# Filler products between scores and values of a Taylor attention, and a DMA wait moved behind the third value store

## The reference

```
k_l = ctx @ Wk_l + bk_l        v_l = ctx @ Wv_l + bv_l        (4096 x 256, l = 0..3)
```

```
s = q.k / 4        weight = 1 + s + s*s/2        out = sum(weight * v) / (sum(weight) + 1e-12)
```

## Time and profile before

| | us |
|---|---|
| median of 3 runs | 1507.49 |
| lowest and highest | 1505.61, 1515.83 |
| the profiled execution's own time | 1513.84 |
| its span | 1512.6 |
| mean granted clock of TensorE in it | 0.958 of 2.4 GHz |

### The profile page before, as it was taken

One profiled execution on the slowest core, in us unless ns is written; L12 is line 12 of the kernel. 1 busy time (PEld: TensorE's weight loads), 2 busy tenths in 40 slices (PEclk: granted clock), 3 DMA queues, 4 the chain that ended last, 5 costly groups with the idle time before them and its releaser, 6 DMA issues. The chain is left out here.

```text
span 1512.6 us, 29029 instructions
## 1 busy us (share of the span) xinstructions
PE 1382.8 (91%) x10576; PEld 812.2 (54%) x10576; DVE 1011.3 (67%) x2314; ACT 857.3 (57%) x1308; POOL 566.7 (37%) x686
## 2 busy tenths in 40 slices
PE   8999798999999988699999888699999897999987
PEld 3765546355555456255555455245555582555555
DVE  4446384999999734778787043498885236888832
ACT  5144140899999721288888542167777211777762
POOL 4565242598989910656555331011111001111100
PEclk9999999799999988799999999889999997999999
DMA  8888987245547053266565094346776711567800
GB/s 265 287 270 247 258 231 246 50 64 85 75 71 155 2 81 44 53 91 88 85 85 144 19 223 171 105 64 102 106 104 209 108 18 45 92 99 105 157 2 8
DMA packets 126008, 178.30 MB, mean 118 GB/s; under 512 B 14733, under 2 KB 106021, under 8 KB 116646
## 3 DMA queue, kind: packets, MB, share of 16 engines
q1 hardware_dynamic: 111898, 161.04, 51.3%
q10 hardware_dynamic: 13968, 15.41, 3.4%
HBM read 132.58 MB, written 43.78 MB: 117 GB/s over the span
## 5 line engine op out<-in xcount | busy, mean ns | idle before, releaser
L1002 ACT ACTIVATE prob_a<-ps 128x1024 f32<-128x1024 f32 x464 | 456.4, 1020 | 143.0 <-PE ps L834 95.7
L817 PE MATMUL ps<-kop,qop 116*128 116x512 bf16 x1024 | 350.3, 406 | 37.3 <-DMA qop<-qparts 24.0
L1026 DVE TENSOR_REDUCE best_a<-ps 128x1 f32<-128x512 f32 (+1 forms) x488 | 318.6, 709 | 49.4 <-PE ps L817 48.9
L834 PE MATMUL ps<-qop,kop 116*128 116x256 bf16 x2048 | 333.9, 274 | 3.2 <-ACT prob_a L1002 2.6
L834 PEld LDWEIGHTS ps<-qop,kop 116*128 116x128 bf16 x2048 | 193.9, 98 | 123.2 <-ACT prob_a L1002 20.2
L1022 DVE CUSTOM_DVE_ANT_0 dump_a<-ps,neg_q 128x512 bf16<-128x512 f32 (+1 forms) x244 | 165.7, 715 | 43.9 <-PE ps L817 41.8
L861 PE MATMUL ps<-prob_a,vop_a 128*32 128x256 f32 x3072 | 191.7, 383 | 3.1 <-POOL prob_a L1166 2.2
L817 PEld LDWEIGHTS ps<-kop,qop 116*128 116x128 bf16 x1024 | 95.6, 103 | 167.0 <-issue 71.0
L1136 POOL TENSOR_TENSOR used_a<-prob_a,gT 128x1024 f32<-128x1024 f32 x64 | 153.1, 2393 | 23.7 <-DVE used_a L1039 18.2
L1115 POOL CAST mpart_a<-nmax_a 128x2 bf16<-128x2 f32 x64 | 26.3, 410 | 353.7 <-DVE nmax_a L1031 353.7
L1166 POOL TENSOR_TENSOR prob_a<-prob_a,neg_k 128x1024 f32<-128x1024 f32 x48 | 102.5, 2135 | 92.0 <-ACT prob_a L1000 86.5
(11 more groups left out here) (337 smaller groups left out, 1830.2 us busy)
## 6 DMA issues: line engine op xcount, KB each, us to landing
kop<-kparts SPq DMA_DIRECT2D x448, 128.0 KB, 5.1
kparts<-kp SPq DMA_DIRECT2D x64, 384.0 KB, 4.7
vals<-vst SPq DMA_DIRECT2D x16, 1024.0 KB, 5.2
vraw<-vals SPq DMA_DIRECT2D x64, 256.0 KB, 6.6
e_w<-in_e_w SPq DMA_DIRECT2D x4, 2048.0 KB, 11.1
z_w<-in_z_w SPq DMA_DIRECT2D x24, 256.0 KB, 6.8
ctxT<-in_ctxT SPq DMA_DIRECT2D x8, 512.0 KB, 8.0
raw<-in_mask ACTq DMA_DIRECT2D x16, 256.0 KB, 5.4
```

The lines of the kernel that those rows point to most:

```text
L817: return pe.matmul(out, qop[0:R_ALL, h, t * P:(t + 1) * P], kop[0:R_ALL, h % UNROLL, j * CHUNK:(j + 1) * CHUNK], start=True, stop=True)
L834: ins = pe.matmul(st_bank(n)[:, j * NT:(j + 1) * NT], kop[0:R_ALL, h % UNROLL, k * P:(k + 1) * P], qop[0:R_ALL, h, :], start=(j % 2 == 0), ...
L1002: act.activation(prob[:, n % NP, :], st_bank(n), ACT.Exp).then_inc(S("exp_done"), 1)
L1026: dve.tensor_reduce(out, bank, AX.X, ALU.max).then_inc(sem, 1)
```

## The change

In the Taylor attention five filler products are issued after scores(0), ahead of values(g) in each of the four rounds, and after the last turn_back, all into bank 0. In the projection stage SP's wait for the blind row's stores, and the load behind it, move from ahead of layer 2's first value store to behind its third.

```diff
-SOFTMAX_FILL, SCAN_FILL = 12, 12
+SOFTMAX_FILL, SCAN_FILL, GROUP_FILL = 12, 12, 5
...
-                if l == 2:
-                    sp.wait_ge(S("blind_stored"), 16 * QT)
-                    sp.dma_start(blind, c.blind_row.rearrange("n o -> o n").to_broadcast((P, NT))).then_inc(S("blind_loaded"), 16)
                 for n in range(NV):
                     b = NV * l + n
                     sp.wait_ge(S("v_staged"), KT * l + VB * (n + 1))
                     sp.dma_start(vout[l, :, n, :, :, :], vst[:, b % VSLOTS, :, :, :])\
                       .then_inc(S(f"v_stored{b % VSLOTS}"), 16)
+                    if l == 2 and n == NV - 2:
+                        sp.wait_ge(S("blind_stored"), 16 * QT)
+                        sp.dma_start(blind, c.blind_row.rearrange("n o -> o n").to_broadcast((P, NT))).then_inc(S("blind_loaded"), 16)
...
             scores(0)
+            keep_warm(c, pe, GROUP_FILL, 0)
             pe.wait_ge(S("v_ready"), 1)
             pe.wait_ge(S("vop_ones"), 1)
             for g in range(G):
                 if g + 1 < G:
                     scores(g + 1)
+                keep_warm(c, pe, GROUP_FILL, 0)
                 values(g)
                 if g >= 1:
                     turn_back(g - 1)
             turn_back(G - 1)
+            keep_warm(c, pe, GROUP_FILL, 0)
             pe.wait_ge(S("normalised"), G)
```

## The result

| | before | after |
|---|---|---|
| median of 20 runs, us | 1511.24 | 1505.64 |
| lowest and highest | 1504.58, 1518.33 | 1501.22, 1511.67 |
| profiled execution, span | 1512.6 | 1503.8 |
| mean granted clock in it | 0.958 | 0.968 |

The ratio of after to before is 0.9967, 95% interval 0.9953 to 0.998: 5.0 us faster, 3.0 to 7.1. The forecast was 7.6 us, with 1493 to 1510 for the time and 1496 to 1504 as the forecast's own range: 1505.64 lies in the first and outside the second. Twenty runs put the median of before at 1511.24, 3.75 us above the median of three on which the forecast's absolute time stood.

The account below looks back on a forecast made before the run. PE at half clock was taken to bound the Taylor rounds, and DVE's 10.02 us store wait layer 2's values. Moved wait -3.1 and fillers -4.5 made -7.6 us: 1507.49 to 1499.9; own range 1496 to 1504, 8 in 10 within 1493 to 1510.

Parts of the forecast that it names:

- A: Taylor stage, between scores and values: clock stays at half and fillers are plain work, +9.8 us, total 1514.2; chance 0.22.
- C: Layer 2's value phase: the moved wait was the whole stall, -10 us, with fillers -4.5, total 1493.0; chance 0.13.
- B: Layer 2's first value store: bounded by the queue, lands at 180 as before; only fillers count, -4.5, total 1503.0; chance 0.15.
- the pieces of a round halve: Taylor rounds: at full clock scores go from 1.61 to 0.8 us, values with turn back from 2.08 to 1.04; rounds give 2.6.
- the clock gives back 0.5 us in the value phase: Layer 2's value phase: PE starts again at about 178.2, at the edge of the clock's fall at 178.5; 0.5 us gained.
- 177.7 instead of 180.34: Layer 2's first value store: lands behind the key store (175.2) plus 2.5 us for 1 MB; DVE's stall shrinks 2.6 us.
- the value store also waits for the factor loads of ACT's queue: Layer 2's first value store: by the ring rule it also waits for ACT's gT pieces, to some 175 to 176.
- the mask conversions: Before layer 3's first mask product: they end at 188.4, before DVE asks at 193.7; cost begins if the gain passes 8 us.
- those packets stay as they were: DMA queue ahead of layer 2's first value store: 105 GB/s from 168 to 172 us, taken as unchanged.

## Why the prediction was right or wrong

*Direction and places: right.* PE at half clock bounded the Taylor rounds, the clock rose with the fillers, the first value store was issued as soon as it could be and landed behind the key store. Rivals A and C are out: the clock stood at 1.00, and DVE waited 6.0 us, not 1. B's sum, 4.5 us, is nearer to the measured 5.0 than mine, but by luck: B had the store land as before and the fillers give 4.5, while the store landed 2.1 us earlier and the fillers gave 3.2. What B had for it, the slow queue, did bound the store: it landed 3.1 us behind the key store, for the 2.5 of my sum.

*The size: too large*, 7.6 for 5.0 (3.0 to 7.1). In the profiled execution -3.2 and -1.3 stand where I had -4.5 and -3.1. Two steps failed: that the pieces of a round halve, and that the clock gives back 0.5 us in the value phase.

*The step of the fillers, "the pieces of a round halve".* The output product gave its 1.7 us. The rounds gave 1.25 us by the last but one turn back (571.06 - 556.84 = 14.2 against 15.5) and not 2.6. One full round, 564.75 to 568.00, is 3.25 us where I had 2.92: values 0.81 for 0.73, turn back 0.37 for 0.31, scores 0.89 for 0.8, fillers 1.18 for 1.08. Every piece is 0.06 to 0.1 us above the half of its time at half clock, which adds up to 0.3 us in a round. And the first fillers delayed scores(1), which ACT paces; values(0) came 5.0 us after the first scores, for 4.4 in my schedule. The tail hid its fillers but for 0.1 us (from the fourth turn back to the turn of the result 1.33 us for 1.23).

*The step of the store, "177.7 instead of 180.34".* It landed at 178.2, 2.1 us earlier for my 2.6 (2.3 counted from the start of the phase), and the wait fell to 6.0. The term that was mis-sized is the clock's: I took 0.5 us gained by a shorter idle time. The idle time did shrink, from 7.51 to 3.52 us, but the clock fell all the same, at 177.8, while PE was idle, and stood at 0.50 for 5.9 us of PE's work behind it, where before it was 4.5: from the restart to the next layer's keys PE took 13.35 us for 12.68, so 0.7 lost. The miss of 1.8 us in this part is then 0.3 from the landing, 1.2 from the clock and 0.3 from layer 3 on. At the beginning of the phase the clock also fell in this execution and not in the one of before; that delays the eighth tile and with it the store. In the kernel before such a fall costs nothing, as the late store hides it (21.1 us from the phase's start to the end of DVE's wait, with the fall and without). I had looked only at the idle time behind the wait. With the clock kept at the beginning the part is 3.9 us, with the fall 0.5 to 1.3. Why the clock falls there in ten of twelve profiles stays open.

*Two readings that changed nothing.* By the prediction the value store also waits for the factor loads of ACT's queue. It didn't: it was issued at 165.36 and landed at 178.2, and the later factor load, issued by 162.0, took 20.0 us and so landed 3 to 4 us behind it. And the mask conversions didn't stay where they were, ending at 188.4, but ended at 194.1, 1.3 us ahead of the first mask product at 195.40; at the 193.7 of the prediction DVE would have met them.

*The base.* The absolute time, 1499.9, was low by 5.7 us: 3.75 of it from a median of three runs that was low, 2.0 from forecasting 7.6 where the medians differ by 5.6. The range of 1493 to 1510 held it, the forecast's own, 1496 to 1504, didn't.

*What I had not asked.* I took the slow stretch of the DMA engines (105 GB/s) as given: "those packets stay as they were". It was the larger item: the wait that the change moves was one symptom of the small stores, and without the stores the stretch is 7.3 to 7.8 us shorter still. The Trainium skill ("DMA: Bandwidth & Descriptors", Specifications) says that transfers under 512 B are read, modified and written; that writes of 4 B are slow agrees with the runs (the value store's 12.5 us with the small stores, 6.9 without), though none shows the reason. That they also hold up another queue's packets is shown by the factor loads of ACT's queue (16.4 us in the median with them, 10.3 without).

The Trainium skill ("TensorE: Matmul & The Clock Gate", Part 1) has the clock follow how busy TensorE is. The runs disagree if busy is what the profile shows: 12.80 of 12.80 us busy at 0.52 with fillers of 16 rows, 11.79 of 12.80 at 1.00 with full ones.

## What to carry to other kernels

Where TensorE is busy with thin products at half clock, a few full products between them can pay: look for the least number that keeps the granted clock through the stage's last large product (three here; two lost it and one never had it, in one profile each), as each one more than that costs time (1.6 us for two more in each group here). When a wait for a DMA is long, ask what made the DMA slow before moving the wait; here a column of single elements stored to DRAM held up a key store, a value store and two loads of another queue, and a product with the identity and ones turns it without a DMA. Changes of a few us are read by the length of the stage where runs spread over 10; whether the kernel gains as much, only the whole runs say, and here they said less in three cases of eight.

## What the runs showed of the hardware that was not expected

256 writes of one element each, 1 KB in all, held both DMA queues to 105 GB/s from 168 to 172 us before the change and to 126 and 167 for eight us after it, against 396 GB/s without them, and made the projection stretch 7.3 us longer in a kernel where nothing in it waits for them. Fillers with 16 rows leave the granted clock at 0.52, with 128 rows at 1.00, at the same count, width and place. Five full fillers in a round gave 1.00 and 20.2 us, three 1.00 and 18.6, one 0.52 and 24.2 (five profiles, two and one). In ten of twelve profiles the clock fell at the beginning of layer 2's value phase, within 1.5 us of PE's return from 3.1 to 3.7 us of idle time; in two it stayed at 1.00 after 3.16 and 2.81 us.
